# Attention's DMA queue: both context loads ahead of the low-half key transposes, and a key semaphore per parity

## The chip, the cores and the metric

One core of one Trainium2 chip runs the whole program. The metric is the device time of one execution, in microseconds (us). A core has TensorE (PE), VectorE (DVE), ScalarE (ACT), GpSimd (POOL) and SyncE (SP), and sixteen DMA engines that they share. Here every DMA is issued by SyncE, one after the other, in program order.

## The reference

It is one decoder layer on x of 16 batches x 256 rows x 2048, in float32, with a context tensor of the same shape. The three stages are:

```
x = layernorm(x + autocorrelation_attention(x))        # FFT correlation, top-7 delays, softmax
sim = softmax((ctx @ x^T) / 16, axis=1)                # per batch, 256 x 256
x = layernorm(x + sim @ ctx)                           # keys and values are the context
x = layernorm(x + x @ W_base^T + moe_lora(x))          # 2048 x 2048, 8 experts of rank 8
```

The kernel does not compute the first attention in full. It takes a layer norm of x in its place, collects for every row what is needed to tell whether that is close enough, and branches to the full path if it is not; the profiled execution does not take that branch.

## The kernel before, in words

`attention_pass` works in slots, n from -2 to 15, with one `batch_slots` loop for each engine. Batch n is 256 rows, as two halves r = 0, 1 of 128 rows. A slot touches three batches at once. For batch n it does the context matmuls (line 643), their eviction (line 522) and the second layer norm. For batch n+1 it turns x on TensorE (lines 625 and 630; evicted as `q_hi` by ScalarE, line 388, and as `q_lo` by VectorE, line 501), computes the logits (line 654), the softmax, and a guard made of matmuls with `fwd` (line 688) and `inv` (line 699), between which ScalarE squares `ps_t` into `power` (line 461). For batch n+2 it loads x, takes its statistics on VectorE (`x_stats`, lines 568 and 573), folds it on GpSimd (line 345), normalises it (GpSimd's `norm1`, lines 315 to 318, and ScalarE's `normalise1`, line 421), and prepares the context. The context is loaded into `cbuf[r]` in float32; ScalarE squares it for a scale (line 399) and then writes `v_hi` (line 455), and VectorE writes the remainder `v_lo` (line 545), both float16. They are the values. The keys are the same numbers turned, which is done by DMA transposes from `v_hi` and `v_lo` into `k_both` (line 247).

`cbuf` has one buffer per half. So the load of batch n+3's half r can go only once `v_lo` of batch n+2's half r has been written (semaphore `vlo_done`). The squares of the newly loaded context stand early in the next slot in ScalarE's program order, between the evictions of the turned x.

SyncE's order in a slot is: the two x2 stores of batch n-1 (line 262; each waits for the normalised half), the load of a weight tile for its sum of squares (line 256), the two x loads of batch n+2 (line 269; each waits for the context evictions of that half of batch n), the two high-half key transposes of batch n+2 (waiting for `v_hi`), and then for each half the low-half transpose (waiting for `v_lo`) and the context load of batch n+3. Slot -2 begins with the first loads instead. TensorE waits at line 671 for the four transposes of a batch, by one semaphore `k_turned` that all of them count up, ahead of the logits. At the end of the pass `w_summed` and `w_reduced` order the sum over the weights between VectorE and GpSimd.

`feed_forward` follows, with 32 tiles of 128 rows, and takes most of the time; its instructions have names ending in `_f`.

Of the kernel before, what the change touches and what calls it, by code (L numbers as in the profile page):

```python
# [35 lines left out]
P = 128  # L36
L = 2048
C = 256
R = C // P
# [80 lines left out]
def attention_pass(nc, src, ctx_in, x2_out, w_chunks, b_rows, ag_in, consts, stored, eps_column, tag):  # L120
# [6 lines left out]
    with ExitStack() as st:  # L127
# [3 lines left out]
        def sem(name):  # L131
            return st.enter_context(nc.semaphore(f"{name}_{tag}"))
# [58 lines left out]
        sumsq_done, sumall_done, scale_ready = sem("sumsq_done"), sem("sumall_done"), sem("scale_ready")  # L191
        t_filled, hi_done, t_free = sem("t_filled"), sem("hi_done"), sem("t_free")
        sim_done, nmax_ready, exp_done, p_ready = sem("sim_done"), sem("nmax_ready"), sem("exp_done"), sem("p_ready")
        vhi_done, vlo_done, k_turned = sem("vhi_done"), sem("vlo_done"), sem("k_turned")
        fwd_done, sq_done, inv_done = sem("fwd_done"), sem("sq_done"), sem("inv_done")
        g_free = [sem(f"g_free{r}") for r in range(R)]
        context_done, ctx_added = sem("context_done"), sem("ctx_added")
        ln2_ready, x2_ready = sem("ln2_ready"), sem("x2_ready")
        dve_step, pool_step = sem("dve_step"), sem("pool_step")
        evac_even, evac_odd = sem("evac_even"), sem("evac_odd")  # L200
        w_loaded, w_squared, w_summed, w_reduced = sem("w_loaded"), sem("w_squared"), sem("w_summed"), sem("w_reduced")
        mv1_ready, mean2_ready, ssq2_ready, mv1_free = sem("mv1_ready"), sem("mean2_ready"), sem("ssq2_ready"), sem("mv1_free")


# [27 lines left out]
        with nc.Block() as block:  # L232
            @block.sync
            def _(sp):
                def load_context(n, r):

                    if is_batch(n, nb):
                        after(sp, vlo_done, R * (n - 1) + r + 1)
                        sp.dma_start(cbuf[r][:], ctx_in[bass.ds(n * C + r * P, P), :]).then_inc(c_loaded[r], 16)

                def transpose_keys(n, parity, part, r):

                    if is_batch(n, nb):
                        if (part, r) == (0, 0):
                            after(sp, sim_done, R * (n - 1))
                        sp.wait_ge((vhi_done, vlo_done)[part], R * n + r + 1)
                        sp.dma_start_transpose(k_both[parity][:, :, part, r * P:(r + 1) * P],
                                               (v_hi, v_lo)[part][parity][:, r]).then_inc(k_turned, 16)

                def load_weights(n):  # L250
                    if is_batch(n, W_TILES):
                        after(sp, w_squared, 2 * n)
                        if isinstance(n, int) and n == 0:
                            sp.dma_start(w_tile[0:ER, :], b_rows).then_inc(w_loaded, 16)
                        else:
                            sp.dma_start(w_tile[:], w_rows[bass.ds((n - 1) * P, P), :]).then_inc(w_loaded, 16)

                def store(n, parity):
                    if is_batch(n, nb):
                        for r in range(R):  # L260
                            sp.wait_ge(x2_ready, R * n + r + 1)
                            sp.dma_start(x2_out[bass.ds(n * C + r * P, P), :], x2buf[parity][:, r]).then_inc(stored[parity][r], 16)

                def load_x(n, parity):
                    if is_batch(n, nb):
                        for r in range(R):

                            after(sp, ctx_added, CG * (n - 2) + NBANK * (r + 1))
                            sp.dma_start(xbuf[parity][:, r], src[bass.ds(n * C + r * P, P), :]).then_inc(x_loaded[parity][r], 16)

                def slot(n, half, parity):
                    if isinstance(n, int) and n == -2:
                        for r in range(R):
                            load_context(0, r)
                        load_x(0, 0)
                        load_weights(0)
                        sp.dma_start(fwd[:], consts["fwd_dram"]).then_inc(tables_loaded, 16)
                        sp.dma_start(inv[:], consts["inv_dram"]).then_inc(tables_loaded, 16)
                    else:
                        store(n - 1, 1 - parity)  # L280
                        load_weights(n + 2)
                        load_x(n + 2, parity)
                    for r in range(R):
                        transpose_keys(n + 2, parity, 0, r)
                    for r in range(R):
                        transpose_keys(n + 2, parity, 1, r)
                        load_context(n + 3, r)

                batch_slots(sp, None, nb, slot, 0)

                sp.wait_ge(stored[0][0], 16)
                sp.wait_ge(w_squared, 2 * W_TILES)
                sp.dma_start(consts["xn0"][:], x2_out[0:P, :]).then_inc(prefetched, 16)
                sp.wait_ge(fwd_done, 4 * nb)
                sp.wait_ge(vlo_done, R * nb)
                sp.dma_start(consts["ag_raw"][:], ag_in.rearrange("p k c -> p (k c)")).then_inc(prefetched, 16)
                for c in range(PREFETCHED):
                    sp.dma_start(consts["chunks"][c].rearrange("p k c -> p (k c)"), chunk_rows(w_chunks, c)).then_inc(prefetched, 16)
                store(nb - 1, (nb - 1) % 2)
                for r in range(R):  # L300
                    sp.wait_ge(stored[0][r], 16 * (nb // 2))
                sp.wait_ge(prefetched, 16 * (PREFETCHED + 2))

            @block.gpsimd
            def _(pool):
                g = nc.gpsimd
# [30 lines left out]
                def slot(n, half, parity):  # L337
                    cur, nxt, n2 = is_batch(n, nb), is_batch(n + 1, nb), is_batch(n + 2, nb)

                    def fold(r):  # L340
                        if n2:
                            if r == 0:
                                after(pool, t_filled, TB * (n + 1) + ORDER.index("u1") + 1)
                            pool.wait_ge(x_loaded[parity][r], 16 * (half + 2))
                            g.tensor_tensor(u_rows[:, r], xbuf[parity][:, r, 0:HALF], xbuf[parity][:, r, HALF:L],
                                            ALU.subtract).then_inc(folded, 1)

                    def norm1(r):
                        if n2:
                            pool.wait_ge(mv1_ready, R * (n + 2) + r + 1)  # L350
                            after(pool, x1_ready[r], n + 2)
                            norm_steps(slice(r, r + 1))

                    if is_batch(n - 1, nb):
                        norm2(n - 1, 1 - parity, 1)
                        normalise2(n - 1, 1 - parity, 1)
                    if cur and n < nb - 1:
                        norm2(n, parity, 0)
                        normalise2(n, parity, 0)
                    fold(0)  # L360
                    norm1(0)
                    fold(1)
                    norm1(1)
                    if n2:
                        chain.link(g.tensor_tensor(mean_sq[:], mv1[:, :, 0], mv1[:, :, 0], ALU.mult))
                        g.tensor_tensor(g_energy[:, bass.ds((n + 2) * R, R)], mean_sq[:], mv1[:, :, 1], ALU.add).then_inc(mv1_free, 1)
                    if n == nb - 1:
                        for r in range(R):
                            norm2(n, parity, r)
                        pool.wait_ge(w_summed, 3)  # L370
                        g.partition_all_reduce(w_total_all[:], w_total[:], P, bass.bass_isa.ReduceOp.add).then_inc(w_reduced, 1)

                batch_slots(pool, chain, nb, slot, 4)

# [102 lines left out]
            def _(dve):  # L477
# [5 lines left out]
                def slot(n, half, parity):  # L483
# [101 lines left out]
                    if isinstance(n, int) and n == nb - 1:  # L585
                        for r in range(R):
                            dve.wait_ge(ln2_ready, R * n + r + 1)
                            v.tensor_scalar(x2buf[parity][:, r], x2buf[parity][:, r], rs2[:, r:r + 1], nb2[:, r:r + 1], ALU.mult,
                                            ALU.add).then_inc(x2_ready, 1)

                        dve.wait_ge(w_squared, 2 * W_TILES)
                        v.tensor_reduce(w_total[:], w_sumsq[:], AX.X, ALU.add).then_inc(w_summed, 1)
                        dve.wait_ge(w_reduced, 1)
                        scale_steps(nc, chain, consts["w_scale"][:], consts["w_iscale"][:], w_total_all[:], tmp[:, 0:1])

                batch_slots(dve, chain, nb, slot, 16)
# [2 lines left out]
            def _(pe):  # L599
                def slot(n, half, parity):  # L600
# [65 lines left out]
                            context_energy()  # L666
                    if nxt:

                        pe.wait_ge(k_turned, 16 * 2 * R * (n + 2))
                        emptied_by, counts, count = emptied(ORDER.index("q3"))  # L670
                        pe.wait_ge(emptied_by, counts * (n + 1) + count)
                        after(pe, g_free[1], n + 1)
# [809 lines left out]
```

## Time and profile before

| | |
|---|---|
| median of 3 runs | 2077.42 us (2074.51 to 2078.51) |
| profiled execution | 2076.62 us |
| its span | 2074.7 us |
| mean granted TensorE clock | 0.991 |
| busy: DVE, ACT, POOL | 855.5, 606.8, 317.1 us |
| moved by DMA | 271.17 MB |

The span runs from the first to the last instruction of the execution; the profiled execution's own time is a little longer. Busy time is the sum over an engine's instructions, so its share of the span says how full the engine is on the average of all stages, not which one ends a given wait. The attention pass takes about the first 590 us, the feed-forward the rest. A slot of the attention pass takes about 34 us.

### The profile page before, as it was taken

The numbers are of one execution on the slowest core, as the hardware profiler recorded it, in microseconds if no ns is written. First come the engines' busy times: TensorE is split into PE (matmuls) and PEld (weight loads), VectorE is DVE, ScalarE is ACT, GpSimd is POOL, SyncE is SP. The second block draws the span as 40 slices with busy tenths as digits, with TensorE's granted clock in tenths as the row PEclk, the third lists the DMA queues.
The fourth block names the chain that finished last, engine by engine and source line by source line (L and its number), as shares of the span: only waits on it lengthen the run. The fifth ranks groups of instructions, "written<-read, shape, count | busy, mean of one in ns | idle before, by whom it ended". The sixth has DMA issues, their size and how long they took to land.

```text
span 2074.7 us, 28253 instructions
## 1 busy us (share of the span) xinstructions
PE 1955.9 (94%) x11264; PEld 1048.8 (51%) x11264; DVE 855.5 (41%) x2167; ACT 606.8 (29%) x771; POOL 317.1 (15%) x529
## 2 busy tenths in 40 slices
PE   3998989898957999999999999999999999999998
PEld 2666666666633444444444444444444444444443
DVE  4777777777757332222232222232222223222221
ACT  5777777777646110000010000011000011000000
POOL 2344444444315000000000000000000000000000
PEclk9999999999979999999999999999999999999999
DMA  8899999999667222111232211123111122221121
GB/s 264 219 291 260 286 261 290 260 294 267 212 216 244 82 92 71 61 61 61 63 102 77 61 61 61 61 91 91 61 61 61 61 80 92 71 61 61 61 61 41
DMA packets 288910, 271.17 MB, mean 131 GB/s; under 512 B 261504, under 2 KB 261632, under 8 KB 265984
## 3 DMA queue, kind: packets, MB, share of 16 engines
q1 hardware_dynamic: 288832, 270.17, 43.7%
q8 instruction: 44, 0.72, 0.1%
q14 instruction: 34, 0.28, 0.0%
HBM read 138.02 MB, written 67.11 MB: 99 GB/s over the span
## 4 chain that ended last, share of the span: by engine, by line
PE 67%; ACT 1%; DVE 1%; DMA 1%; POOL 1%; issue 0%; ACTq 0%; POOLq 0%
PE ps_y_f L1117 62%; PE ps_a_f L1136 2%; PE ps_y_f L1121 1%; PE ps_y_f L1122 1%; PE ps_a_f L1137 1%; ACT w_hi_f L912 1%; DMA cbuf<-w_chunks 0%; DVE w_lo_f L986 0%; DMA chunk<-w_chunks 0%; POOL w_lo_f L895 0%; POOL cbuf L894 0%; PE ps_h_f L1144 0%; DVE b_stack_f L1072 0%; ACT y_f L973 0%; PE ps_t_f L1102 0%
## 5 line engine op out<-in xcount | busy, mean ns | idle before, releaser
L1117 PE MATMUL ps_y_f<-w_hi_f,x_hi_f 128*128 128x512 f16 x2048 | 777.8, 380 | 10.9 <-POOL w_lo_f L895 8.1
L1117 PE MATMUL ps_y_f<-w_hi_f,x_lo_f 128*128 128x512 f16 x2048 | 777.9, 380 | 0.0
L1117 PE MATMUL ps_y_f<-w_lo_f,x_hi_f 128*128 128x512 f16 x2048 | 777.7, 380 | 0.0
L973 ACT ACTIVATE y_f<-y_f,nb_f,rs_f 128x2048 f32<-128x2048 f32 x32 | 67.0, 2094 | 1112.3 <-POOL nb_f L903 1112.3
L1117 PEld LDWEIGHTS ps_y_f<-w_hi_f,x_hi_f 128*128 128x128 f16 x2048 | 200.6, 98 | 248.5 <-POOL w_lo_f L895 10.6
L1117 PEld LDWEIGHTS ps_y_f<-w_hi_f,x_lo_f 128*128 128x128 f16 x2048 | 200.7, 98 | 242.6 <-issue 1.7
L1117 PEld LDWEIGHTS ps_y_f<-w_lo_f,x_hi_f 128*128 128x128 f16 x2048 | 200.7, 98 | 233.7 <-issue 1.4
L997 DVE SCALAR_TENSOR_TENSOR y_f<-ps_y_f,w_iscale,xn_f 128x512 f32<-128x512 f32 x64 | 46.6, 748 | 476.6 <-PE ps_y_f L1122 476.6
L997 DVE SCALAR_TENSOR_TENSOR y_f<-ps_y_f,w_iscale,xn 128x512 f32<-128x512 f32 x64 | 46.5, 748 | 448.5 <-PE ps_y_f L1122 448.5
L900 POOL TENSOR_TENSOR var_eps_f<-mv_f,columns 128x1 f32<-128x1 f32 x32 | 6.0, 189 | 1357.0 <-DVE mv_f L1085 1357.0
L654 PE MATMUL ps_s_fast<-k_both_fast,q_hi_fast 128*128 128x256 f16 x1024 | 169.9, 274 | 0.0
L654 PE MATMUL ps_s_fast<-k_both_fast,q_lo_fast 128*128 128x256 f16 x512 | 140.2, 274 | 0.0
L522 DVE SCALAR_TENSOR_TENSOR x2buf_fast<-ps_c_fast,iscale_fast,xbuf_fast 128x512 f32<-128x512 f32 x128 | 95.9, 750 | 71.4 <-PE ps_c_fast L643 70.6
L501 DVE TENSOR_TENSOR q_lo_fast<-ps_t_fast,q_hi_fast 128x512 f16<-128x512 f32 x128 | 86.4, 686 | 59.1 <-ACT q_hi_fast L388 58.9
L654 PEld LDWEIGHTS ps_s_fast<-k_both_fast,q_hi_fast 128*128 128x128 f16 x1024 | 100.8, 98 | 15.2
L625 PE MATMUL ps_t_fast<-ident,xbuf_fast 128*128 128x128 f32 x512 | 76.1, 284 | 23.1 <-DVE q_lo_fast L501 10.1
L643 PE MATMUL ps_c_fast<-v_hi_fast,p_lo_fast 128*128 128x512 f16 x256 | 97.0, 379 | 0.0
L643 PE MATMUL ps_c_fast<-v_lo_fast,p_hi_fast 128*128 128x512 f16 x256 | 97.0, 379 | 0.0
L643 PE MATMUL ps_c_fast<-v_hi_fast,p_hi_fast 128*128 128x512 f16 x256 | 97.0, 379 | 0.0
L625 PEld LDWEIGHTS ps_t_fast<-ident,xbuf_fast 128*128 128x128 f32 x512 | 63.1, 146 | 46.5 <-DVE q_lo_fast L501 19.0
L1013 DVE BATCH_NORM_STATS2 stats_f<-y_f 128x6 f32<-128x512 f32 x128 | 85.3, 687 | 2.2
L688 PE MATMUL ps_t_fast<-ag_raw,fwd_fast 128*128 128x256 bf16 x512 | 60.9, 273 | 23.6 <-ACT power_fast L461 23.6
(160 smaller groups left out, 2083.9 us busy)
## 6 DMA issues: line engine op xcount, KB each, us to landing
xbuf_fast<-x SPq DMA_DIRECT2D x32, 1024.0 KB, 7.8
x_scratch<-x2buf_fast SPq DMA_DIRECT2D x32, 1024.0 KB, 6.3
out<-y_f SPq DMA_DIRECT2D x32, 1024.0 KB, 4.0
cbuf<-ctx_in SPq DMA_DIRECT2D x16, 1024.0 KB, 5.7
cbuf_fast<-ctx_in SPq DMA_DIRECT2D x16, 1024.0 KB, 6.8
xn<-w_chunks SPq DMA_DIRECT2D x16, 1024.0 KB, 7.7
xn<-x_scratch SPq DMA_DIRECT2D x16, 1024.0 KB, 4.7
xn_f<-x_scratch SPq DMA_DIRECT2D x16, 1024.0 KB, 4.8
```

What stands on the lines that cost most here:

```text
L501: v.tensor_tensor(q_lo[at], bank, q_hi[at], ALU.subtract).then_inc(t_free, 1)
L522: v.scalar_tensor_tensor(x2buf[parity][:, r, b * BANK:(b + 1) * BANK], ps_c[j % 2][:], iscale[parity][:], xbuf[parity][:, r, b * BANK:(b + ...
L625: ins = nc.tensor.transpose(bank[:, i * P:(i + 1) * P], xbuf[other][:, r, (kk + i) * P:(kk + i + 1) * P], ident[:])
L643: ins = nc.tensor.matmul(ps_c[j % 2][:], pp[:, d, r * P:(r + 1) * P], vv[parity][:, d, b * BANK:(b + 1) * BANK], start=(i == 0), stop=(i = ...
L654: ins = nc.tensor.matmul(ps_s[r][:, 0:C], qq[:, k, r * P:(r + 1) * P], k_both[other][:, k, part, :], start=(i == 0), stop=(i == 3 * KT - 1))
L688: ins = nc.tensor.matmul(ps_t[m % 3][:, 0:C], fwd[:, k, m * P:(m + 1) * P], u_t[:, k, :], start=(k == 0), stop=(k == HALF // P - 1))
L912: nc.scalar.activation(w_hi[chunk_at(c)], chunk[buffer_of[c]], ACT.Copy, scale=w_scale[:]).then_inc(w_hi_done, 1)
L973: nc.scalar.activation(y[parity][:], y[parity][:], ACT.Identity, bias=nb_[:, 0:1], scale=rs[:, 0:1]).then_inc(out_ready, 1)
L997: v.scalar_tensor_tensor(y[parity][:, at], ps_y[j][:], w_iscale[:], xn[parity][:, at], ALU.mult, ALU.add).then_inc(evacuated, 1)
L1013: return v.bn_stats(stats[:, j], y[parity][:, j * BANK:(j + 1) * BANK])
L1117: nc.tensor.matmul(ps_y[j][:], xx[parity][:, k], ww[:, k, j * BANK:(j + 1) * BANK], start=(k == 0 and xx is x_hi and ww is w_hi), stop=False)
L1136: nc.tensor.matmul(ps_a[:, 0:2 * AG], x_hi[parity][:, k], ag_t[:, k, :], start=(k == 0), stop=False)
```

## The change

In SyncE's slot both context loads are issued after the high-half transposes and ahead of both low-half transposes. `k_turned` becomes a list of two semaphores, one for each parity of the batch, and TensorE waits for the one of batch n+1, whose count is 64 for each batch of that parity so far. `w_reduced` is dropped: GpSimd's all-reduce counts `w_summed` to 4, and VectorE waits for that.

```
-        vhi_done, vlo_done, k_turned = sem("vhi_done"), sem("vlo_done"), sem("k_turned")
+        vhi_done, vlo_done = sem("vhi_done"), sem("vlo_done")
+        k_turned = [sem(f"k_turned{i}") for i in range(2)]
...
-        w_loaded, w_squared, w_summed, w_reduced = sem("w_loaded"), sem("w_squared"), sem("w_summed"), sem("w_reduced")
+        w_loaded, w_squared, w_summed = sem("w_loaded"), sem("w_squared"), sem("w_summed")
...
                         sp.dma_start_transpose(k_both[parity][:, :, part, r * P:(r + 1) * P],
-                                               (v_hi, v_lo)[part][parity][:, r]).then_inc(k_turned, 16)
+                                               (v_hi, v_lo)[part][parity][:, r]).then_inc(k_turned[parity], 16)
...
                     for r in range(R):
                         transpose_keys(n + 2, parity, 0, r)
                     for r in range(R):
+                        load_context(n + 3, r)
+                    for r in range(R):
                         transpose_keys(n + 2, parity, 1, r)
-                        load_context(n + 3, r)
...
-                        g.partition_all_reduce(w_total_all[:], w_total[:], P, bass.bass_isa.ReduceOp.add).then_inc(w_reduced, 1)
+                        g.partition_all_reduce(w_total_all[:], w_total[:], P, bass.bass_isa.ReduceOp.add).then_inc(w_summed, 1)
...
-                        dve.wait_ge(w_reduced, 1)
+                        dve.wait_ge(w_summed, 4)
...
-                        pe.wait_ge(k_turned, 16 * 2 * R * (n + 2))
+                        pe.wait_ge(k_turned[1 - parity], 16 * 2 * R * ((n + 1) // 2 + 1))
```

## Rows read from the trace of the kernel before

**Rows 1.** The page, part 1: busy us (share of the span) x instructions.

```profile
PE 1955.9 (94%) x11264; PEld 1048.8 (51%) x11264; DVE 855.5 (41%) x2167; ACT 606.8 (29%) x771; POOL 317.1 (15%) x529
```

**Rows 2.** Waits of TensorE, 0 to 700 us: total us, times, longest.

```profile
PE ps_t_fast L688 <- ACT power_fast L461: 23.6, 14, 2.3
```

**Rows 3.** Timeline of SyncE, start-up: start us, us, instruction, tiles.

```profile
24.61 2.98 SPq L247 DMA_TRANSPOSE k_both_fast<-v_lo_fast  x1
27.64 0.62 SPq L239 DMA_DIRECT2D cbuf<-ctx_in  x1
28.32 5.59 SPq L247 DMA_TRANSPOSE k_both_fast<-v_lo_fast  x1
33.95 0.58 SPq L239 DMA_DIRECT2D cbuf_fast<-ctx_in  x1
```

**Rows 4.** Timeline, the other engines, start-up; brackets: idle before, what ended it.

```profile
22.61 2.96 DVE L545 SCALAR_TENSOR_TENSOR v_lo_fast<-cbuf_fast,scale_fast,v_hi_fast 128x2048 f16<-128x2048 f32 x1
...
34.15 1.06 ACT L399 ACTIVATE junk_fast<-cbuf 128x1024 bf16<-128x1024 f32 x1 [4.40 <-DMA cbuf<-ctx_in]
...
40.51 1.06 ACT L399 ACTIVATE junk_fast<-cbuf_fast 128x1024 bf16<-128x1024 f32 x1 [3.21 <-DMA cbuf_fast<-ctx_in]
...
45.58 2.35 POOL L345 TENSOR_TENSOR u_rows_fast<-xbuf_fast 128x1024 bf16<-128x1024 f32 x1 [18.51 <-DMA xbuf_fast<-x]
...
48.82 2.46 DVE L568 BATCH_NORM_STATS2 stats_fast<-xbuf_fast 128x6 f32<-128x512 f32 x4
...
58.79 3.66 PE L688 MATMUL ps_t_fast<-ag_raw,fwd_fast 128*128 128x256 bf16 x32
```

**Rows 5.** Windows: window, us, busy of each engine, PEclk, DMA share, GB/s.

```profile
40.00:45.00 5.00, 1.24 (x5) 0.84 (x6) 0.87 (x2) 4.07 (x7) 0.00 (x0) 1.00 1.00 424
```

**Rows 6.** Timeline of SyncE, a typical slot's end and the next one's beginning.

```profile
331.81 2.62 SPq L247 DMA_TRANSPOSE k_both_fast<-v_lo_fast  x1
334.48 0.58 SPq L239 DMA_DIRECT2D cbuf<-ctx_in  x1
...
337.92 2.79 SPq L247 DMA_TRANSPOSE k_both_fast<-v_lo_fast  x1
340.76 0.57 SPq L239 DMA_DIRECT2D cbuf_fast<-ctx_in  x1
341.38 6.71 SPq L262 DMA_DIRECT2D x_scratch<-x2buf_fast  x2
348.13 0.43 SPq L256 DMA_DIRECT2D xn<-w_chunks  x1
349.86 7.67 SPq L269 DMA_DIRECT2D xbuf_fast<-x  x2
```

**Rows 7.** Line 239 (context loads), 60 to 540 us.

```profile
DMA to landing us min/median/max: 5.2/6.7/7.3
```

**Rows 8.** Landing: line 247 (60 to 540 us), then x loads issued at 349.86, 176.52.

```profile
DMA to landing us min/median/max: 4.2/4.8/6.9
...
xbuf_fast<-x SPq DMA_DIRECT2D x1, 1024.0 KB, 8.3
...
xbuf_fast<-x SPq DMA_DIRECT2D x1, 1024.0 KB, 10.2
```

**Rows 9.** Timeline: typical slot (356, 359 us), slots 2 and 3; a window.

```profile
356.22 0.38 PE L654 MATMUL ps_s_fast<-k_both_fast,q_hi_fast 128*128 128x256 f16 x2
...
359.24 2.46 DVE L568 BATCH_NORM_STATS2 stats_fast<-xbuf_fast 128x6 f32<-128x512 f32 x4
...
175.04 1.06 ACT L399 ACTIVATE junk_fast<-cbuf_fast 128x1024 bf16<-128x1024 f32 x1 [1.33 <-DMA cbuf_fast<-ctx_in]
...
186.76 1.88 DVE L568 BATCH_NORM_STATS2 stats_fast<-xbuf_fast 128x6 f32<-128x512 f32 x3 [0.59 <-DMA xbuf_fast<-x]
...
198.65 1.05 PE L688 MATMUL ps_t_fast<-ag_raw,fwd_fast 128*128 128x256 bf16 x8 [2.33 <-ACT power_fast L461]
...
200.00:204.00 4.00, 3.76 (x13) 1.75 (x14) 0.55 (x2) 2.16 (x2) 0.00 (x0) 0.57 1.15 225
```

## The prediction

> **What bounds the kernel now.** I read the page's shares first: TensorE is busy for 94% of 2074.7 us [rows 1], so what moves the end is TensorE's idle time. Next the waits, TensorE alone, up to 700 us: no wait on a key transpose and none on a context load appears; the largest is the fourth block of `fwd` matmuls waiting for ScalarE's guard squares, 23.6 us in 14 slots [rows 2]. Then SyncE's queue in order of time, at the start [rows 3] and in a typical slot [rows 6], beside the other engines in the same stretches [rows 4, 9]: there the loads do end waits, of engines that stand ahead of TensorE. The feed-forward behind it is not touched and moves as a block.
>
> Names: H0, H1, L0, L1 are the high and low key transposes of the two row halves, C0 and C1 the context loads, S0 and S1 the x2 stores, W the weight load, X0 and X1 the x loads. The queue was H0 H1 L0 C0 L1 C1; it becomes H0 H1 C0 C1 L0 L1. C1 (and L1) wait for v_lo of half 1, so L0 now stands behind a wait that it did not have.
>
> **Start-up.** v_lo of half 1 ends at 22.61 + 2.96 = 25.57 [rows 4]. H1 is issued by 24.61, then came L0, C0 at 27.64, L1 for 5.59 us, C1 at 33.95 [rows 3]. C0 now goes at 24.6 (3.0 earlier), C1 at 25.6 (8.3 earlier). ScalarE idled 4.40 us for C0, until 34.15, and 3.21 us for C1, until 40.51 [rows 4]; TensorE's transposes waited behind it. Both idles go: with 4.5 us from a transpose's landing to that of the load behind it and 2.5 us for the next one, C0 lands near 31.5 and C1 near 34. (2.5 us is 1024 KB at the 424 GB/s of 40 to 45 us, where the DMA share is 1.00 [rows 5].) ScalarE's order from C1's first square to the logits (6.4 us: 40.51 to 46.9, 58.79 less the 11.9 of two logits [rows 4]) then puts the logits at about 41, some 6 us early.
>
> What is late next is X0. It landed at 45.58, ending GpSimd's 18.51 us of idle [rows 4]; DMA was full until then [rows 5], and the order within a full queue does not change when the last of the same bytes lands. VectorE took x's statistics at 48.82; it can now do so at 45.5. From there a chain runs without slack: statistics, GpSimd's norm1, ScalarE's normalise1, exponentials and guard squares, then TensorE. So the start gains 48.82 - 45.5 = 3.3 us and not 6. The ends: 2 us if the transposes, now last, keep X0 back by 1.3; 4.7 us if X0 lands 1.4 earlier since one idle stretch between transpose and load is gone. I take 3.4. The keys of batch 0, formerly landed by 36, land near 38.5 to 40.5; TensorE wants them at 41, with 3 us more before they would count, since the logits end early.
>
> **Steady slots, C1.** C1 goes at 337.92 instead of 340.76 [rows 6], 2.8 us earlier, and lands by 343 or 344 where it landed at 347.5; the square that needs it starts at 347. ScalarE waited for it in 11 of 13 slots, 0.3 to 1.4 us. What that costs I read from TensorE's slots: waits up to 1.1 us cost nothing (slots of 34.13 us with 0.3 and with 1.1); only slots 2 and 3, with 1.35 and 1.33 [rows 9], made slots of 34.34 and 34.31, some 0.2 us each. Gain 0.4 us. Its ends are 0 and 0.7 (against the 33.99 of the slots without any wait).
>
> **Steady slots, the transposes.** Each transpose's issue lasts until the transfer ahead of it has landed: L1 issued at 28.32 for 5.59 us ends at 33.91, C0 (landing 6.5 us after 27.64) at 34.1 [rows 3]; in the typical slot 340.71, and C0, 5.7 us after its issue, 340.2 [rows 6]. Nine slots agree to 0.3 us. So with L0 behind C1 its issue lasts to 343.1 (C1's shortest landing, 5.2 us [rows 7]), L1's to about 345.3, and L1 lands at 347.5 (4.4 us [rows 8]). TensorE reads these keys at 356.22 [rows 9]: 8.7 us of slack, no cost; with a landing of 6.9 [rows 8] still 6. S0 moves from 341.38 to 345.4. S1 waits for x2 until 347.7 anyway and W and X0 stand behind it, with X0 issued at 349.86 as before [rows 6]. SyncE's queue itself is thus covered, by 1.9 us; if that cover went, W would be late, then X0.
>
> The transfers are less covered. X0 lands 8.3 us after its issue, at 358.2 [rows 8]; VectorE wants it at 359.24 [rows 9]. The slack is 1.0 us. In front of it stand now, behind L1 at 347.5, S0, S1, W and X0: four at 2.5 us give 357.5, 0.7 earlier than before. With 1.3 us lost between transpose and plain transfer (C0 landed 3.8 after L0 in this slot) it is 358.8; with the stores at 2.8 instead of 2.5 it is 359.4, 0.2 too late. I take 358.6: late by 0.4, hidden by the slack. What lateness costs is in the trace: in slot 3, X0 took 10.2 us [rows 8], VectorE waited 0.59, TensorE's wait for the guard squares rose to 2.33, and after it the granted clock was 0.57 for 200 to 204 us (in that stretch it was at the lower of its two levels, 1.2 GHz, for most of the time) [rows 9]. The slot took 36.55 us, 2.4 over 34.13, of which 0.7 is X0 and 1.6 the clock.
>
> The order of landing in every row here is the order of issue. The Trainium skill (DMA: Bandwidth & Descriptors, Queues, rings and completion order) has descriptors of one engine's ring consumed in ring order; that speaks against the change, as the moved transposes stay ahead of X0. By it alone my 358.6 stands, and the case below in which X0 is late is what it would give if the transfers take the longer times. [...]
>
> **The semaphores.** The key wait takes all four transposes of batch n+1, by the parity's own count instead of the whole; `w_reduced` becomes the fourth count of `w_summed`. The same instructions end the same waits: 0, and it is not above 0.1 us, for TensorE had no key wait.
>
> **Sum.** The profiled execution took 2076.6 us (span 2074.7), 0.8 below the median 2077.4. 2076.6 - 3.4 - 0.4 = 2072.8; from the median, 2073.6. I forecast 2073.6.
>
> **Rivals.**
> A, the forecast, 0.44: start-up's 3.4 and 0.4, X0 hidden. Range 2071.5 to 2075.5.
> B, slot 3's late X0 vanishes too, 0.14: before, L1 and C1 went out late in slots 2 and 3 (C1 0.9 later in its slot than usual) because L1 waited for C0; C1 goes by v_lo alone now. Another 2.3: 2071.3. Against it: slots 2 and 3 were slow in the transfers themselves.
> C, X0 late in a few slots, 0.22: the scatter of X0 is 7.8 to 10.2 us; with 0.4 on top two or three slots pass 9.4. Two more slots of 2.0 give the gain back: 2077.5.
> D, the other side, 0.20: X0 late in most slots. One mechanism: the low transposes, held behind C1, push S0, S1, W and X0 back past VectorE's statistics. It decides once X0 moves by over 1.0 us; at 1.6 it costs 0.6 in each of 13 slots, 7.8, with two clock drops of 1.6: 2077.4 - 3.8 + 7.8 + 3.2 = 2084.6; at 1.2 about 2079. For it: DMA is full in most of each slot. Against it: the bare rate gives 357.5.
> That the change does nothing (the start-up gain eaten elsewhere) is within C.
>
> **Chances.** 0.2% of the time, 4.2 us, is what a measurement can tell from no change: faster is below 2073.2. A gives 0.19 faster, 0.25 same; B 0.14 faster; C 0.03 faster, 0.15 same, 0.04 slower; D 0.02 same, 0.18 slower. Together 0.36, 0.42, 0.22. The range 2070.5 to 2081.5 takes in B, C and D's lesser half; A's own is 2071.5 to 2075.5.
>
> **What would show it.** Right: C0 and C1 issued near 24.6 and 25.6, no ScalarE wait for C0 or C1 above 1 us, the first logits near 41, slot 0 starting near 61.3 (before 64.66), x's statistics in a typical slot 17.6 us after the first context matmul as before, slots of 34.13 us. Wrong: VectorE waiting for x in many slots; X0 landing over 9.4 us after its issue; the wait for the guard squares above 1.7 us per slot; more stretches of low clock; a TensorE wait on the keys. Had L0's issue not waited for C1's landing, the transposes' step is wrong.

## The result and the profile after

The changed kernel takes 2080.77 us in the median of 8 runs (2078.58 to 2085.85), the kernel before 2074.47 in 8 (2073.35 to 2078.51): ratio 1.0031, 95% interval 1.0022 to 1.0040, slower by some 6 us. The forecast was 2073.6, faster or no change. The profiled executions lie closer, 2078.58 (span 2076.7) against 2076.62: that of the changed kernel is its fastest run, that of the kernel before is slower than six of its eight. The traces explain the 2.0 us between the spans; what the medians add is taken up at the end.

The waits of the attention pass come first (total us, times, longest), TensorE's, VectorE's for x, ScalarE's for the context, in the changed kernel; they answer to [rows 2].

```profile
PE ps_t_fast L690 <- ACT power_fast L463: 30.5, 15, 2.8
...
DVE stats_fast L570 <- DMA xbuf_fast<-x: 7.1, 9, 1.9
...
ACT junk_fast L401 <- DMA cbuf<-ctx_in: 4.5, 2, 3.6
```

ScalarE's wait for the second context load, 12.8 us before, is gone, and the wait for the first is down to 0.9 in slot -1. In their place VectorE waits for x nine times, once in slot -1 and in eight later slots (once, 0.6 us, before), and TensorE's wait for the guard squares has grown by 6.9 us. Next the start-up, SyncE's timeline and then the other engines, beside [rows 3, 4].

```profile
24.61 0.97 SPq L240 DMA_DIRECT2D cbuf<-ctx_in  x1
25.63 0.44 SPq L240 DMA_DIRECT2D cbuf_fast<-ctx_in  x1
26.11 9.11 SPq L248 DMA_TRANSPOSE k_both_fast<-v_lo_fast  x2
```

```profile
30.54 1.06 ACT L401 ACTIVATE junk_fast<-cbuf 128x1024 bf16<-128x1024 f32 x1 [0.90 <-DMA cbuf<-ctx_in]
...
39.99 0.59 PE L656 MATMUL ps_s_fast<-k_both_fast,q_hi_fast 128*128 128x256 f16 x2
...
43.91 2.47 DVE L570 BATCH_NORM_STATS2 stats_fast<-xbuf_fast 128x6 f32<-128x512 f32 x4 [1.94 <-DMA xbuf_fast<-x]
```

The loads go out at the times forecast, the logits start at 40.0, and VectorE now waits for x, from 42.0 to 43.9. Slot 0 starts at 59.06 where it started at 64.66. The start gained 5.6 us. (A slot is counted from TensorE's first transpose of the next batch's x.)

Then a typical slot's end: SyncE's timeline from slot 8 into slot 9, beside [rows 6]; and the landing of its x load, beside [rows 8].

```profile
364.50 0.92 SPq L240 DMA_DIRECT2D cbuf<-ctx_in  x1
370.80 0.33 SPq L240 DMA_DIRECT2D cbuf_fast<-ctx_in  x1
371.18 7.09 SPq L248 DMA_TRANSPOSE k_both_fast<-v_lo_fast  x2
378.31 2.62 SPq L263 DMA_DIRECT2D x_scratch<-x2buf_fast  x2
380.98 1.14 SPq L257 DMA_DIRECT2D xn<-w_chunks  x1
```

```profile
368.44 2.34 DVE L547 SCALAR_TENSOR_TENSOR v_lo_fast<-cbuf_fast,scale_fast,v_hi_fast 128x2048 f16<-128x2048 f32 x1
```

```profile
xbuf_fast<-x SPq DMA_DIRECT2D x1, 1024.0 KB, 9.9
```

C0 is out by 365.4; SyncE then stands still until v_lo of half 1 (written by 368.44 + 2.34 = 370.78) allows C1 at 370.80. L0 stands behind it, though its own v_lo, that of half 0, was written by 362.9. The next windows show what the DMA engines do in that time (window, us, busy of PE, PEld, DVE, ACT, POOL, granted clock, DMA share, GB/s), first the changed kernel and then the kernel before, its slot laid over it:

```profile
366.00:368.00 2.00, 2.00 (x20) 1.65 (x17) 1.89 (x8) 1.91 (x6) 1.75 (x7) 1.00 1.02 270
368.00:370.00 2.00, 0.28 (x3) 0.16 (x3) 1.96 (x3) 2.00 (x7) 0.00 (x0) 1.00 0.65 270
370.00:372.00 2.00, 1.46 (x11) 0.85 (x10) 1.69 (x4) 1.35 (x4) 0.00 (x0) 1.00 0.51 53
372.00:374.00 2.00, 2.00 (x15) 1.38 (x13) 0.00 (x0) 1.55 (x2) 0.00 (x0) 1.00 0.62 233
```

```profile
367.50:369.50 2.00, 1.98 (x19) 1.53 (x16) 1.89 (x6) 1.91 (x5) 1.76 (x7) 1.00 1.14 211
369.50:371.50 2.00, 0.38 (x4) 0.35 (x5) 1.97 (x3) 2.00 (x7) 0.14 (x1) 1.00 1.11 210
371.50:373.50 2.00, 1.46 (x11) 0.76 (x9) 1.43 (x4) 1.35 (x3) 0.00 (x0) 1.00 1.01 389
373.50:375.50 2.00, 2.00 (x16) 1.50 (x14) 0.00 (x0) 1.55 (x2) 0.00 (x0) 1.00 1.15 251
```

From 368 to 374 us the DMA share is 0.5 to 0.65, where it had been full with L0. (The share counts a packet by its start, so it can pass 1.) It is so in every slot: over the 6 us that end 0.85 us after a slot's start, the share is 0.42 to 0.73 in slots 2 to 12 of the changed kernel, and 1.01 to 1.15 in those of the kernel before. That work is done later, ahead of the stores, the weights and x. What it leads to stands in the timelines of VectorE and TensorE of the changed kernel, beside [rows 9]: slot 9, then slot 3.

```profile
392.67 1.29 DVE L570 BATCH_NORM_STATS2 stats_fast<-xbuf_fast 128x6 f32<-128x512 f32 x2 [0.51 <-DMA xbuf_fast<-x]
```

```profile
193.83 1.05 PE L690 MATMUL ps_t_fast<-ag_raw,fwd_fast 128*128 128x256 bf16 x8 [2.31 <-ACT power_fast L463]
195.41 1.82 PE L701 MATMUL ps_g_fast<-inv_fast,power_fast 128*128 128x512 bf16 x4 [0.54 <-ACT power_fast L463]
197.03 1.91 PE L701 MATMUL ps_s_fast<-inv_fast,power_fast 128*128 128x512 bf16 x4
```

The two groups of four `inv` matmuls take 1.8 and 1.9 us here and 1.04 and 1.03 at the full clock: they ran at 1.2 GHz, the lower of the two levels (granted clock 0.50 from 195.5 to 198.9 us).

From slot 0's start to slot 14's the kernel before took 545.08 - 64.66 = 480.42 us, the changed one 547.83 - 59.06 = 488.77, 8.35 more. TensorE's guard waits explain 5.3 of it (6.9, less the 1.6 of slot -1, which lies ahead of slot 0), three stretches of low clock (slots 3, 6, 10; 1.6, 1.6 and 1.7 us) where there was one of 1.6 another 3.3, and C1's gain takes off 0.4: together 8.2 of the 8.35. The start took 5.6 less and what follows slot 14's start, the feed-forward above all, 0.75 less. Over the whole span, 8.35 - 5.6 - 0.75 = 2.0, the difference of the spans.

### The profile page after: what moved, and what is told of

Read it like the earlier page. It is cut to its first block, busy times and chain, and to the rows that moved or that the text cites. A ratio compares the mean times of both kernels' runs of the same rounds, so it can differ in the third digit from the quotient of the medians.

```text
span 2076.7 us, 28253 instructions
## 1 busy us (share of the span) xinstructions
PE 1957.0 (94%) x11264; PEld 1048.1 (50%) x11264; DVE 857.4 (41%) x2167; ACT 604.6 (29%) x771; POOL 316.9 (15%) x529
## 4 chain that ended last, share of the span: by engine, by line
PE 67%; ACT 1%; DVE 1%; DMA 1%; POOL 0%; issue 0%; ACTq 0%; POOLq 0%
PE ps_y_f L1119 62%; PE ps_a_f L1138 2%; PE ps_y_f L1123 1%; PE ps_y_f L1124 1%; PE ps_a_f L1139 1%; ACT w_hi_f L914 1%; DMA chunk<-w_chunks 1%; DVE w_lo_f L988 0%; DMA cbuf<-w_chunks 0%; PE ps_h_f L1146 0%; POOL cbuf L896 0%; POOL w_lo_f L897 0%; DVE b_stack_f L1074 0%; ACT y_f L975 0%; PE ps_t_f L1104 0%
```

## The experiments

Theory Q: L0, held behind C1's wait, leaves the DMA engines idle and puts its work ahead of x. Rivals: P, the shift of the start brings the slots into a bad phase; R, a transpose behind C1 costs, since its issue lasts until C1 has landed; S, the semaphores. Each ratio is against the kernel before run on the same chip, of 2076.3, 2077.4 and 2077.6 us in the three groups (e1 to e4, e5 to e8, e9 and e10), and gains and losses against it are given by the ratio.

**e1, the semaphores alone.** The old loop with `k_turned[parity]` and `w_summed` counted to 4:

```
                     for r in range(R):
+                        transpose_keys(n + 2, parity, 1, r)
                         load_context(n + 3, r)
-                    for r in range(R):
-                        transpose_keys(n + 2, parity, 1, r)
```

> The queue order of the kernel before, with the changed kernel's semaphores alone (a key semaphore per parity, w_summed counted to 4). Theory Q (the low transposes held behind the second context load's wait push the x load back): the semaphores are nothing, so the time is that of the kernel before, within 0.1%, statistics never or once late for x, one or no clock drop. Theory S (the semaphores or their counts cost something): between the two kernels or at the changed one's 2080.

2077.7 us, ratio 1.0003 (0.9994 to 1.0011). The time is that of the kernel before, and the interval leaves room for a cost of 2.3 us at most. S falls as the cause of the 11 us that e3 shows. The trace has two late x loads (0.7 and 1.0 us) and two falls of the clock, one more of each than was expected, with the old order in every slot: both occur without the change too.

**e2 and e3, the order in one stage alone.** e2 has the changed order in slot -2 and the old one later; e3 the reverse:

```
+                    if n == -2:        # e3: if n != -2
                         for r in range(R):
                             load_context(n + 3, r)
                         for r in range(R):
                             transpose_keys(n + 2, parity, 1, r)
+                    else:
+                        for r in range(R):
+                            transpose_keys(n + 2, parity, 1, r)
+                            load_context(n + 3, r)
```

> The changed queue order in slot -2 alone, the old order in all later slots, the changed semaphores. Theory Q: slot 0 starts near 59.1 as in the changed kernel (5.6 earlier than before), later slots take 34.1 as before; some 5.6 us below the kernel before, 2069 where that has 2074.5. Rival P (the start-up shift itself brings the slots into a bad phase, whatever the later order): the x loads are late here too, and the time is 2077 to 2081.

> The old order in slot -2, the changed order in all later slots. Theory Q: slot 0 starts near 64.7 as before, statistics late for x in most slots, about 8 us and the clock drops on top of the changed order's steady part: some 10 to 12 us above the kernel before, 2085 to 2087. Rival P (the start-up shift is the cause): at the time of the kernel before, 2074.5.

e2: 2070.8 us, ratio 0.9973 (0.9963 to 0.9983), 5.6 us faster; slot 0 starts at 58.6, VectorE waits for x in one later slot. e3: 2089.0 us, ratio 1.0055 (1.0042 to 1.0068), 11.4 slower; slot 0 starts at 64.6, and VectorE waits in eight slots (total, times, longest). The median is 2 us above the 2085 to 2087 expected:

```profile
DVE stats_fast L575 <- DMA xbuf_fast<-x: 6.1, 8, 1.1
```

So one edit holds a gain of 5.6 us and a loss of 11 (12.7 by the medians). The changed kernel's 6 is their sum. P falls: the shift without the order costs nothing, the order costs without the shift.

**e4, 1 MB less ahead of the first x load.** The changed kernel with the weight load between the two x loads:

```
-                        load_weights(n + 2)
-                        load_x(n + 2, parity)
+                        load_x(n + 2, parity, (0,))
+                        load_weights(n + 2)
+                        load_x(n + 2, parity, (1,))
```

> The changed kernel with the weight load moved from ahead of the first x load to between the two x loads: 1 MB less ahead of the first x load. Theory Q: the first x load lands 1.5 to 2.5 us earlier after its issue (7.5 to 8.5 in place of 9.9 us), VectorE no longer waits for it, the wait for the guard squares is 1.6 us in every slot and the clock stays up; the start-up gain of 5.6 us is left over: 2067 to 2070. Rival T (lateness comes from the transposes' own interference, not from the bytes ahead): less than 2 us below the changed kernel's 2080.

2067.82 us, ratio 0.9957 (0.9944 to 0.9970). The low transposes are where the changed kernel has them, and their issue still lasts 7.1 us; x lands 7.4 us after its issue in slot 9 and never over 7.9, VectorE waits for it in no slot after -1, and TensorE's guard waits are (total, times, longest):

```profile
PE ps_t_fast L697 <- ACT power_fast L470: 22.9, 14, 1.6
```

The DMA share around a slot's start is as low as in the changed kernel (0.54 to 0.71, the same 6 us, slots 2 to 12). So the loss of the steady slots is all in x's landing: with that early, the late transposes, the late stores and the keys cost nothing that shows. The clock still fell once, in slot 0 (granted 0.57 from 89 to 93 us), after the usual wait of 1.63 us. So a low clock does not need a late x.

**e5 and e6, L0 or C1.** Both have the changed order in slot -2. Later slots, e5 and then e6:

```
+                        transpose_keys(n + 2, parity, 1, 0)     # e5: H0 H1 L0 C0 C1 L1
+                        for r in range(R):
+                            load_context(n + 3, r)
+                        transpose_keys(n + 2, parity, 1, 1)
...
+                        for r in range(R):                      # e6: H0 H1 C0 L0 C1 L1
+                            load_context(n + 3, r)
+                            transpose_keys(n + 2, parity, 1, r)
```

> The changed order in slot -2; in all later slots H0 H1 L0 C0 C1 L1: the first low transpose back in its old place, the second context load still ahead of the second low transpose. Theory Q (it is L0 held behind the wait of C1): nothing but C1 and L1 is left for after v_lo of half 1, as before, so the x load lands 8 to 9 us after its issue and VectorE waits at most once or twice: 2069 to 2072. Rival R (a transpose behind C1 is what costs, since its issue lasts until C1 has landed): the x loads land near 9.5 us, late in half of the slots, and the time is 2076 to 2080.

> The changed order in slot -2; in all later slots H0 H1 C0 L0 C1 L1: each context load ahead of the transpose of its own half. L0 then waits for v_lo of half 0 alone, and its issue for C0's landing, which comes about when v_lo of half 1 is ready. Theory Q: L0 still fills the DMA engines' idle time ahead of C1, at most 0.5 us of it is left for later: 2069 to 2073, as with L0 first. Rival R (transposes behind context loads cost): 2076 to 2080.

e5: 2070.86 us, ratio 0.9970 (0.9960 to 0.9981). e6: 2068.32, ratio 0.9961 (0.9948 to 0.9975). In both C1 goes ahead of L1, as in the changed kernel, and ScalarE does not wait for it. x lands 7.7 to 9.7 us after its issue in slots 1 to 13. VectorE waits in none of these slots of e5 and in one of e6, 0.2 us. R falls. SyncE's timeline of e6, and the windows in which the changed kernel's share was low:

```profile
359.88 0.92 SPq L240 DMA_DIRECT2D cbuf<-ctx_in  x1
360.84 5.61 SPq L248 DMA_TRANSPOSE k_both_fast<-v_lo_fast  x1
366.49 0.57 SPq L240 DMA_DIRECT2D cbuf_fast<-ctx_in  x1
367.11 5.31 SPq L248 DMA_TRANSPOSE k_both_fast<-v_lo_fast  x1
372.47 3.36 SPq L263 DMA_DIRECT2D x_scratch<-x2buf_fast  x2
```

```profile
363.00:365.00 2.00, 0.35 (x4) 0.27 (x4) 1.96 (x3) 2.00 (x7) 0.00 (x0) 1.00 1.00 356
365.00:367.00 2.00, 1.46 (x11) 0.79 (x10) 1.57 (x4) 1.35 (x3) 0.00 (x0) 1.00 1.12 226
```

L0 is issued 6 us ahead of C1, in the time in which the changed kernel's queue stood still. C1 goes when L0's issue ends, 0.8 us after its v_lo was ready (365.65) and so 0.8 us later in its slot than in the changed kernel, which costs nothing here. Only the place of L0 differs from the changed kernel, and with it the DMA engines stay busy: over the same 6 us of slots 2 to 12 the share is 1.02 to 1.17 (e5: 0.92 to 1.08).

**e7 to e9, the weight load moved as well.** To e2, e5 and e6, each with e4's edit:

> The changed order in slot -2, the old order in all later slots, and the weight load between the two x loads. Theory Q: the x load lands 5.5 to 7 us after its issue, in every slot early enough; what is left are the slots' 34.13 us, so 2066 to 2069, 1 to 3 us below the same kernel with the weight load in its old place, which had one or two late x loads. Rival N (with the weight load moved the order of the transposes does not matter, and the two kernels with it are alike, 2067.8): the same number, so the two are told apart only by the landing, 1.5 us earlier here than with the changed order.

> The changed order in slot -2, H0 H1 L0 C0 C1 L1 in all later slots, and the weight load between the two x loads: no wait of ScalarE for the context and no wait of VectorE for x. Theory Q: 34.13 us in every slot from 2 on, 2066 to 2068. Rival: the clock falls once or twice whatever the waits are, as it did once in slot 0 of the changed order with the weight load moved, and the time stays within 1 us of that kernel's 2067.8.

> The changed order in slot -2, H0 H1 C0 L0 C1 L1 in all later slots, and the weight load between the two x loads. Both kernels that it is made of were near 2068. Theory Q: the x load is early in every slot, so only the slots' own 34.13 us and the clock drops are left: 2066 to 2068, within 1 us of the three kernels with the weight load moved. Rival (the two edits add up, since each takes away another wait): 2064 to 2066.

e7: 2068.54 us, ratio 0.9962 (0.9949 to 0.9976); e8: 2067.32, 0.9956 (0.9942 to 0.9969); e9: 2067.16, 0.9957 (0.9944 to 0.9969). VectorE waits for x in no slot after -1 in any. The five kernels with 0.9956 to 0.9962 (e4, e6 to e9) can't be told apart; they beat the kernel before by 8 to 9 us. With x early already, moving W behind X0 adds nothing that shows to L0 in its idle time, as Q expects, and the rival that the two gains add up (2064 to 2066) falls with e9. In e7, x lands 6.0 to 8.0 us after its issue (slots 1 to 13), 0.4 us earlier in the median than in e4 where 1.5 was expected. e7 leaves ScalarE 12.4 us of waits for the second context load and loses nothing by them that can be seen here.

**e10, the changed kernel once more.**

> The changed kernel itself, its queue order only written in two branches, on the chip of the run beside it: a second trace of it. Theory Q: x's statistics late in at least six of the slots 1 to 12 by 0.4 to 1.1 us, two to four clock drops, slot 0 starting near 59; 2079 to 2084, some 12 to 15 us above the kernel run beside it. Rival (the first trace was an unlucky one): late in three slots or fewer and below 2076.

2081.68 us, ratio 1.0022 (1.0012 to 1.0033), 14.5 us above e9 on the same chip, as theory Q expects. Its trace has VectorE's waits again (total, times, longest; the first is slot -1's, the other eight are late x loads of later slots):

```profile
DVE stats_fast L576 <- DMA xbuf_fast<-x: 7.6, 9, 1.8
```

and five stretches of low clock, one more than expected. In the traces with the changed order in the steady slots and the weight load in its place there are 3, 4 (e3) and 5; in the nine others, that of the kernel before among them, 0 to 2 (two with none, six with one, one with two).

## Why the prediction was wrong

- **Start-up, forecast -3.4: right in mechanism, too small.** Measured -5.6 by the trace, and -5.6 by e2 (its interval, 3.5 to 7.7 us). C0, C1, the logits and x's role as the next thing late came as worked out. The term mis-sized was x's landing: I argued that a full queue lands the same bytes at the same time and took 45.5; it landed at 43.9, 7.5 us after its issue. The idle time between a transpose and the load behind it, named as the end of the range, occurs once less. That moves VectorE's statistics by 48.82 - 43.91 = 4.9 us; the other 0.7 is likely TensorE's own, as its logits ended only at 58.8 before and it waited for no squares in the `fwd` matmuls of that slot, while now it waits 1.62 us. This share was not tested apart.
- **C1, -0.4:** the waits went. Half of it can be seen: slot 2 took 34.33 us before, with a wait of 1.35, and 34.13 in e9 without. e5 against e2 (0.9970 and 0.9973) shows no gain beyond the intervals.
- **Transposes' issue and the keys: right.** L0 and L1 were issued until 7.5 us after C1 (forecast 7.4); TensorE never waited for keys; S1, W and X0 were issued as before.
- **x's landing in the steady slots: the step that failed.** I put it at 8.8 us after issue, within a slack of 1.0 us behind 8.3, and took lateness as hidden. It is 9.8 to 10.5 us in eight of thirteen slots. In slot 9 C1 landed 5.7 us after its issue instead of the 5.2 taken, which was the shortest in any slot before; S0 landed at 383.7, S1 at 387.5, W at 389.9, X0 at 392.6. The two stores are 3.8 us apart (2.3 to 4.4 in the other slots where S1 is issued behind S0 within 2.5 us) where I had 2.5, the rate of loads, in the sum (2.8 was in the range). The landing missed by 9.9 - 8.8 = 1.1 us: C1 is 0.5 of it and the second store 3.8 - 2.5 = 1.3; from C1 to S0 it took 383.7 - 376.5 = 7.2 where I had allowed 8.0, 0.8 less, and W and X0 together 0.1 more.
- **The choice.** I took the middle of the ends 0.8 earlier and 1.2 later and called it hidden, though the cost is not even-handed: an early x gains nothing, a late one costs all of it, with the clock's 1.6 us behind. Rival D named the mechanism, its point of decision and both prices, with a chance of 0.20; the low clock came three to five times in its traces where I had put two. What I had weighed too little is that L0 had filled idle DMA time, visible in SyncE's timeline of before: it was issued at 331.81 and C1's wait ended at 337.9.
- **The direction.** The forecast said faster or no change, and the kernel is slower. The median of 2080.77 lies inside the range given (2070.5 to 2081.5), by luck in part: two terms were missed in opposite directions, and with the start at the 3.4 forecast it would be 2083.

What stays open: why the clock falls in some slots and not in others with the same waits (510 us in the changed kernel: a wait of 2.82 us, and the full clock after it). The runs of the changed kernel spread over 7 us, and the medians lie 6.3 apart where the traces lie 2.0. Each run's mean granted clock is on record and does not explain it: the two slowest (2085.5 and 2085.9) had 0.988, while 0.985, the lowest, went with 2079.8 and 2081.2. What else varies from run to run stays open, as only the profiled executions can be read by stage.

## What to carry to other kernels

In a queue served in order, an entry moved behind one that must wait takes its own work out of idle time and puts it ahead of everything later: ask what the moved entry had been filling, and where the next load with little slack stands. Put each entry behind the wait that it needs and no other (C0 L0 C1 L1), and move a transfer that nobody awaits behind the one that somebody does. An edit made for all slots may gain in the first and lose in the rest: weigh the stages one by one.

## What the runs showed of the hardware

- A DMA transpose's issue on SyncE lasts until the transfer ahead of it has landed: in e6 all 29 transposes issued right behind a context load ended their issue 0.15 to 0.3 us ahead of its landing. Two behind C1 took 6.9 to 7.4 us in eleven of thirteen slots of the changed kernel (8.4 and 9.2 in the others), one behind a load mostly 5.3 to 5.6 (e6), against 2.2 to 3.7 for L0 behind H1 in the kernel before. In slot 9 of the changed kernel S0 was issued 7.5 us after C1.
- Two stores of 1 MB that queue behind one another landed 3.6 us apart in the median of ten slots of the changed kernel (2.3 to 4.4), loads 2.5 (W to X0: 2.5 to 2.8 in eleven of thirteen slots, 3.3 and 3.9 in the others).
- In all twelve traces every transfer that SyncE issued landed in the order of issue, transposes included.
- The granted clock fell to 1.2 GHz for some 3.5 us in the guard's stage 0 to 5 times in an attention pass, each time within 3 us of TensorE's wait for the squares. Over the twelve traces it fell after 13 of the 28 such waits of over 2 us (2.1 to 2.8), and after 7 of the 140 shorter ones (the seven were of 1.63 to 1.65 us, in e1, e4 to e8 and e10). Each time it cost 1.5 to 1.7 us.
